# Cross attention on one core: maximum scores in one pair of PSUM banks, read by one VectorE operation of 616 columns, in place of two single banks and operations of 308

## What is computed

```
Q = x @ Wq.T + bq ; K = ctx @ Wk.T + bk ; V = ctx @ Wv.T + bv
scores = Q K^T / sqrt(16) ; attn = softmax(scores) ; context = attn @ V
y = context @ Wo.T + bo + x
out = (y - mean(y)) / sqrt(var(y) + 1e-5) * gamma + beta
```

## Time and profile before

| | us |
|---|---|
| median of three executions | 227.6 |
| profiled execution | 227.75 |
| its span | 225.9 |
| TensorE busy | 203.4 |
| GpSimd busy | 183.9 |
| VectorE busy | 181.3 |
| ScalarE busy | 172.0 |

### The profile page before, as it was taken

How to read it: one execution, slowest core, us unless ns; L and a number is a source line. 1 busy time by engine, 2 the same in 40 slices (tenths; PEclk the granted TensorE clock), 3 DMA queues, 4 the chain that set the end, 5 groups by cost and what they waited for, 6 DMA issues and landing times.

```text
span 225.9 us, 6883 instructions
## 1 busy us (share of the span) xinstructions
PE 203.4 (90%) x2740; PEld 190.3 (84%) x2740; DVE 181.3 (80%) x378; ACT 172.0 (76%) x313; POOL 183.9 (81%) x163
## 2 busy tenths in 40 slices
PE   0999999899999899989999899989998999999830
PEld 0997799799999789988999799969997999998720
DVE  5699977468778978987988888897889788885494
ACT  4589579778879769896889688968896887887530
POOL 9999464786388958997699869985999499999973
PEclk9999999999999999999999999999999999999995
DMA  6947321434721153115321432143124111211022
GB/s 204 328 79 208 63 55 52 149 99 154 201 65 46 49 147 98 51 52 138 94 59 49 128 70 90 52 124 80 50 72 80 46 49 49 78 65 49 0 96 93
DMA packets 24808, 20.96 MB, mean 93 GB/s; under 512 B 10554, under 2 KB 21953, under 8 KB 24776
## 3 DMA queue, kind: packets, MB, share of 16 engines
q1 hardware_dynamic: 23544, 19.26, 30.3%
q10 hardware_dynamic: 1232, 1.26, 1.9%
HBM read 11.32 MB, written 4.19 MB: 69 GB/s over the span
## 4 chain that ended last, share of the span: by engine, by line
POOL 35%; PE 29%; DVE 12%; issue 12%; ACT 8%; DMA 2%; POOLq 0%; DVEq 0%; ACTq 0%
POOL p_l L1046 22%; PE ps_x L348 12%; PE ps_s L348 8%; DVE xT_l L768 6%; PE ps_acc L348 5%; POOL result L1054 5%; POOL x_rows L1063 4%; POOL rs_y L1075 3%; PE ps_d L348 3%; ACT p_h L688 3%; DVE result L909 2%; DMA w_raw<-in_wkT 2%; ACT ctx_h L695 1%; POOL rs_v L1069 1%; DVE vrest L800 1%
## 5 line engine op out<-in xcount | busy, mean ns | idle before, releaser
L1046 POOL TENSOR_TENSOR p_l<-p,p_h 128x512 f16<-128x512 f32 x80 | 100.6, 1264 | 29.0 <-ACT p_h L688 28.1
L854 DVE TENSOR_REDUCE maxima<-ps_d 128x4 f32<-128x308 f32 x128 | 57.2, 465 | 12.0 <-PE ps_d L348 10.8
L687 ACT ACTIVATE p<-ps_s 128x512 f32<-128x512 f32 x80 | 47.5, 594 | 18.0 <-PE ps_s L348 16.9
L348 PE MATMUL ps_s<-q_low,kblk 128*128 128x256 f32 x192 | 47.5, 282 | 1.1 <-issue 1.0
L348 PE MATMUL ps_acc<-vblk,p_h 128*128 128x34 bf16 (+1 forms) x960 | 47.0, 182 | 0.5 <-POOL p_l L1046 0.4
L688 ACT ACTIVATE p_h<-ps_s 128x512 f16<-128x512 f32 x80 | 47.3, 591 | 0.0
L348 PEld LDWEIGHTS ps_acc<-vblk,p_h 128*128 128x128 f16 x960 | 42.6, 96 | 4.8 <-issue 1.9
L348 PE MATMUL ps_acc<-vblk,p_l 128*128 128x34 bf16 (+1 forms) x640 | 45.1, 181 | 0.0
L348 PE MATMUL ps_s<-q_lo,kblk 128*128 128x256 f32 x160 | 45.0, 281 | 0.0
L348 PE MATMUL ps_d<-kblk,q_low 128*128 128x308 f32 x128 | 41.6, 329 | 0.2 <-DVE maxima L854 0.2
L348 PEld LDWEIGHTS ps_acc<-vblk,p_l 128*128 128x128 f16 x640 | 38.7, 96 | 0.0
(11 more groups left out here) (90 smaller groups left out, 458.8 us busy)
## 6 DMA issues: line engine op xcount, KB each, us to landing
xT_raw<-in_xT SPq DMA_DIRECT2D x8, 512.0 KB, 3.9
x_rows<-in_x SPq DMA_DIRECT2D x16, 256.0 KB, 2.9
out_dram<-result SPq DMA_DIRECT2D x15, 256.0 KB, 2.2
kblk<-kT SPq DMA_DIRECT2D x64, 38.5 KB, 2.3
c_raw<-in_cT ACTq DMA_DIRECT2D x4, 308.0 KB, 3.9
vblk<-vparts SPq DMA_DIRECT2D x4, 184.1 KB
rows_sb<-in_bias_rows SPq DMA_DIRECT2D x1, 384.0 KB, 6.4
kblk<-kblk SPq DMA_DIRECT2D x3, 96.0 KB, 2.4
```

What stands on the lines that cost most here:

```text
L348: return nc.tensor.matmul(o, w, m, start=start, stop=stop, skip_group_check=True)
L687: nc.scalar.activation(p32[:, n % P32SLOTS], ps_s[n % 2][:], ACT.Exp, scale=SCALE)
L854: v_.tensor_reduce(maxima[:, t, h0:h0 + DMAX_HEADS], ps_d[((DMAX + 1) * (s + 1) + j) % 2][:, 0:DMAX_HEADS * SKV] .rearrange("p (h k) -> p ...
L1046: g_.tensor_tensor(p_l[:, n % PSLOTS], p32[:, n % P32SLOTS], p_h[:, n % PSLOTS], ALU.subtract).then_inc(rest16, 1)
```

## The change

The two banks become one tile of two banks (ps_d, 128 x 2 x 512). DMAX goes from 8 to 4: for each query tile and half, two matmuls (308 columns each, the same queries) fill both banks back to back, the second one signals, and one VectorE operation reduces the 616 columns to eight maxima. A pair of matmuls waits until the reduction of the pair before is done, since no other bank is left. The table tasks has one entry for all steps: pairs 0, 1, 2 and 3 at (0, 0), (1, 1), (2, 0) and (3, 1). On VectorE reductions 0 and 1 and reductions 2 and 3 of before become one each, ahead of and behind the residual; the third pair comes between the denominators of half 1 and aggregate, the fourth behind the normalization of half 1. In the last output step (s = 16) the second half of the turned context uses the first bank of the pair, and the turned maxima lie there too.

```diff
--- before.py
+++ after.py
@@ -58,7 +58,7 @@
 WIDE = TILES * P
 UNITS = HALVES * TILES // 2
 DMAX_HEADS = HH // 2
-DMAX = QT * HALVES * 2
+DMAX = QT * HALVES
 VW = DK + 1
 VP = 3
 GROUP = 4
@@ -196,7 +196,7 @@
 
         ps_s = [bank(f"ps_s{n}", [P, 2, SQ]) for n in range(2)]
         ps_acc = [bank(f"ps_acc{n}", [P, 512]) for n in range(2)]
-        ps_d = [bank(f"ps_d{n}", [P, 512]) for n in range(2)]
+        ps_d = bank("ps_d", [P, 2, 512])
         ps_x = [bank(f"ps_x{n}", [P, 512]) for n in range(2)]
 
 
@@ -250,7 +250,7 @@
 
         def context_turned(s, f):
 
-            return (ps_d[0], 0) if s == B and f else (ps_x[0], f * SQ)
+            return (ps_d[:, 0], 0) if s == B and f else (ps_x[0][:], f * SQ)
 
 
         low_rows, high_rows = slice(P - MROWS, P), slice(0, MROWS)
@@ -417,31 +417,27 @@
                 s = S.first
                 nb = s + 1
 
-                def max_bank(j):
-                    return ps_d[((DMAX + 1) * nb + j) % 2]
-
                 def max_scores(j):
 
-                    t, f, n = j // 4, j // 2 % 2, j % 2
+                    t, f = divmod(j, HALVES)
                     if j == 0:
                         if nb % 2 == 0:
                             S.wait(pe, ld_k[nb // 2 % 2], 16 * HH, 16 * HH * (5 - nb % 4), by=4)
                             S.wait(pe, q_hi, 1, 3)
-                        S.wait(pe, max_done, DMAX, DMAX)
-                    elif j == 1:
                         S.wait(pe, m_done, 1, 1)
                     else:
-                        S.wait(pe, max_done, DMAX, DMAX + j - 1)
+                        S.wait(pe, max_done, DMAX, DMAX + j)
                     q0 = nb % 2 * SQ + t * P
-                    mm(max_bank(j)[:, 0:DMAX_HEADS * SKV], q_low[nb // 2 % 2][:, f, q0:q0 + P],
-                       kblk[:, nb % KSLOTS, f, 0, n * DMAX_HEADS * SKV:(n + 1) * DMAX_HEADS * SKV],
-                       True, True).then_inc(pe_d, 1)
+                    for n in range(2):
+                        ins = mm(ps_d[:, n, 0:DMAX_HEADS * SKV], q_low[nb // 2 % 2][:, f, q0:q0 + P],
+                                 kblk[:, nb % KSLOTS, f, 0, n * DMAX_HEADS * SKV:(n + 1) * DMAX_HEADS * SKV], True, True)
+                    ins.then_inc(pe_d, 1)
 
                 def turn_maxima():
 
                     S.wait(pe, max_done, DMAX, 2 * DMAX)
                     for t in range(QT):
-                        ins = nc.tensor.transpose(max_bank(DMAX)[0:MROWS, t * P:(t + 1) * P], maxima[:, t, :], ident_sb[:])
+                        ins = nc.tensor.transpose(ps_d[0:MROWS, 0, t * P:(t + 1) * P], maxima[:, t, :], ident_sb[:])
                     ins.then_inc(pe_m, 1)
 
                 def score_tile(u, n):
@@ -541,11 +537,7 @@
 
 
 
-                tasks = {(0, 0): 0, (0, 1): 1, (1, 0): 2, (1, 1): 3, (2, 0): 4, (2, 1): 5, (3, 0): 6, (3, 1): 7,
-                         (4, 1): DMAX}
-                if S.project_q and s > 0:
-                    tasks = {(0, 0): 0, (0, 1): 1, (0, 2): 2, (1, 0): 3, (1, 2): 4, (2, 0): 5, (2, 2): 6, (3, 1): 7,
-                             (4, 1): DMAX}
+                tasks = {(0, 0): 0, (1, 1): 1, (2, 0): 2, (3, 1): 3, (4, 1): DMAX}
                 for u in range(UNITS):
                     for part in range(4):
                         if part < 2 and S.scores:
@@ -702,7 +694,7 @@
                         act.wait_ge(shift_set, 1)
                     nb = s + 1
                     cols = slice(nb % 2 * SQ, (nb % 2 + 1) * SQ)
-                    m = ps_d[((DMAX + 1) * nb + DMAX) % 2][0:MROWS, 0:SQ].unsqueeze(1).broadcast_to([MROWS, HALVES, SQ])
+                    m = ps_d[0:MROWS, 0, 0:SQ].unsqueeze(1).broadcast_to([MROWS, HALVES, SQ])
                     nc.scalar.activation(q_low[nb // 2 % 2][low_rows, :, cols], m, add, bias=shift[low_rows, 0:1])
                     nc.scalar.activation(q_high[nb // 2 % 2][high_rows, :, cols], m, add,
                                          bias=shift[high_rows, 0:1]).then_inc(m_done, 1)
@@ -846,14 +838,13 @@
 
                 def max_of(j):
 
-                    t, f, n = j // 4, j // 2 % 2, j % 2
+                    t, f = divmod(j, HALVES)
                     S.wait(dve, pe_d, DMAX, DMAX + j + 1)
                     if j == 0:
                         S.wait(dve, pe_m, 1, 1)
-                    h0 = f * HH + n * DMAX_HEADS
-                    v_.tensor_reduce(maxima[:, t, h0:h0 + DMAX_HEADS],
-                                     ps_d[((DMAX + 1) * (s + 1) + j) % 2][:, 0:DMAX_HEADS * SKV]
-                                     .rearrange("p (h k) -> p h k", k=SKV), AX.X, ALU.max).then_inc(max_done, 1)
+                    v_.tensor_reduce(maxima[:, t, f * HH:(f + 1) * HH].rearrange("p (n h) -> p n h", n=2),
+                                     ps_d[:, :, 0:DMAX_HEADS * SKV].rearrange("p n (h k) -> p n h k", k=SKV),
+                                     AX.X, ALU.max).then_inc(max_done, 1)
                     if j in between:
                         between[j]()
 
@@ -948,14 +939,12 @@
                 when(S.output, (denominators, 0))
                 when(S.maxima, (max_of, 0))
                 when(S.output, (normalize, 0))
-                when(S.maxima, (max_of, 1))
                 when(s == B, (denominators, 1), (normalize, 1))
                 when(S.norm, (residual,))
                 when(s == B, (context_lo_part, 0))
-                when(S.maxima, (max_of, 2))
+                when(S.maxima, (max_of, 1))
                 if S.norm:
                     S.wait(dve, y_done, 1, -1)
-                when(S.maxima, (max_of, 3))
                 when(S.norm, (statistics, 0))
                 when(S.project_q, (queries, 0))
                 when(s == B, (context_lo_part, 1))
@@ -964,14 +953,11 @@
                 when(s == B - 1, (bias_x,))
                 if S.norm:
                     S.wait(dve, stats_done, QT, -QT)
-                when(S.maxima, (max_of, 4))
+                when(S.maxima, (max_of, 2))
                 when(S.norm, (aggregate,))
-                when(S.project_q, (max_of, 5))
                 when(S.output and s < B, (normalize, 1))
                 when(S.project_q, (queries, 1))
-                when(S.maxima and not S.project_q, (max_of, 5))
-                when(S.maxima, (max_of, 6))
-                when(S.maxima, (max_of, 7))
+                when(S.maxima, (max_of, 3))
                 when(S.output and s < B, (context_lo_part, 0, 1))
                 when(S.norm, (centre, 0), (centre, 1))
                 if S.split_x:
@@ -992,7 +978,7 @@
                 dve.wait_ge(x_hi, 2)
                 split_x()
 
-            step(Step(-1), {1: split_second_x, 3: lambda: (value_rest(3), context_lo(3)), 5: lambda: key_lo(2)})
+            step(Step(-1), {0: split_second_x, 1: lambda: (value_rest(3), context_lo(3)), 2: lambda: key_lo(2)})
             values(2)
             key_lo(3)
             weight_lo(3)
```

## The result

The changed kernel took 231.26 us, the profiled execution included, and the kernel before 227.57 to 227.60 in the runs of the same comparison; the ratio is 1.0161, with a 95% interval from 1.0136 to 1.0185. That is 1.6% slower: less than the 2% that were set as the bound for a change, but well clear of no difference, and 0.7 us over the forecast of 230.6 us. (Both kernels also have executions some 2% longer at a lower granted clock, 0.974 and 0.983 in place of 0.99 for the changed one, and the times and ratios compared from here on leave such executions out.)

What follows compares the result with a forecast made beforehand. TensorE was taken as nearly full and VectorE as having room; -0.2, +0.32 (step 1), +0.37 (step 2), +2.1 (steps 3 to 12) and +0.32 (step 13) make +2.9 us, forecast 230.6 us, 8-in-10 range 227.5 to 233.3.

Steps and rivals of the forecast that it cites:

- up to the start of step 1: Step -1: shorter reductions bring the keys' low part and projection forward, 0.2 us gained; step 0 has no transposes, nothing.
- step 1: Odd step with no later wait as cover: transposes wait for the normalization, 0.32 us paid in full.
- step 2: Even step with no wait ahead to absorb or move: transposes wait for the normalization, +0.37 us.
- steps 3 to 12: Five pairs of an odd and an even step, each +0.42 us from late transposes, together +2.1 us.
- step 13: Odd step with no later wait for xT_l as cover: late transposes cost +0.32 us in full.
- step 14: Its delay falls into TensorE's 0.44 us wait for GpSimd in step 15 and costs nothing.
- The start of the third reduction: On VectorE, a reduction can start some 0.35 us behind the start of its matmul.
- If ctx_l no longer waits for ScalarE in the odd step: Sign of being wrong: VectorE's 0.70 us idle ahead of ctx_l in the odd step would be gone.
- A longer reduction: Longer by x costs 13x at most: x in steps 1, 2, 4, 6, 8, 10, 12, 3x in 13 and 14.
- no change: Rival: waits ahead of the transposes don't arise or the third reduction starts sooner; 227.6 us, chance 0.14.
- faster (VectorE bounds): Rival: VectorE's 3.8 us come off the path, chiefly as less waiting for xT_l; 223.8 us, chance 0.06.
- The slower one: Rival: one operation over two banks takes longer than its columns say; over 2% slower, 233.4 us at 0.90 us, chance 0.20.

Runs made afterwards that it cites:

- experiment 5: Changed kernel with the merging undone, each pair reduced by two operations of 308 columns, all else kept: 232.74, 232.91 and 234.15 us, ratio 1.0227.
- experiment 3: Changed kernel with the normalization of half 1 ahead of the third reduction in odd steps 3 to 11 alone: 231.26 to 231.68 us, ratio 1.0161.
- experiment 2: Changed kernel with the normalization of half 1 ahead of the third reduction in even steps 0 to 12 alone: 227.92 to 230.44 us, ratio 1.0038.
- experiment 1: Changed kernel with the normalization of half 1 ahead of the third reduction and aggregate in every step: 227.03 to 228.20 us, ratio 0.9993.
- experiment 7: Kernel before, unmerged, with the normalization of half 1 moved behind one more reduction on VectorE: 230.47 to 231.15 us, ratio 1.0119.
- Experiment 4: Changed kernel with the normalization of half 1 ahead of the third reduction in step 14 alone: 231.07 to 231.28 us, ratio 1.0148.
- experiment 6: Changed kernel reducing only the first 48 of a head's 77 keys, 384 columns in place of 616: 228.10 to 229.10 us, ratio 1.0023.
- experiment 8: Changed kernel with the normalization ahead of the third reduction in every step and xT_l ahead of centre in odd steps: 230.48 and 231.13 us, ratio 1.0119.

## Why the prediction was right, and where it was off

The mechanism held. TensorE has little room, VectorE has much; the merged operation is priced by its columns (forecast 0.71 us of spacing and 0.79 of duration, measured 0.72 and 0.79) and gives back some 0.06 us a pair, as the gaps of experiment 5 confirm (0.70 against 0.64 us); the transposes wait for a normalization that stands behind it; and the loss of odd steps 3 to 11 is covered by the wait for xT_l (experiment 3) while that of the even ones is paid (experiment 2). Experiments 1 and 7 show the cause from both sides: take the late normalization out of the change and its loss is gone, put it into the kernel before and 2.9 us are lost. Two steps take 23.89 us (138.52 to 162.41), forecast 23.87.

The sum was 2.9 us; the profiled executions differ by 3.5 and their spans by 3.6. Term by term, as forecast and as measured: up to the start of step 1, -0.2 and -0.29; step 1, +0.32 and +0.40; step 2, +0.37 and +0.46; steps 3 to 12, +2.1 and +2.30 (0.57 to 2.87); step 13, +0.32 and +0.39; step 14, nothing and +0.40, of which the last stretch takes back 0.09 to the end of the span. The first term fits by luck: 0.2 us were forecast for step -1 and nothing for step 0, and it was 0.09 ahead of step 0 and 0.20 within it. What gained the 0.20 is open.

- **Step 14** is the term that failed, and the largest part of the difference. I had let its delay fall into TensorE's wait for GpSimd in step 15. That wait is 0.43 us in the trace of the change, as before: what it waits for came later too. Experiment 4 gives some 0.3 us for step 14. The idle time of one engine is cover only if the engine it waits for is not itself delayed.
- **The start of the third reduction and the length of the transposes** are the mis-sized terms in the other steps. I let a reduction start 0.35 us behind its matmul; from step 2 on the third one starts 0.41 us behind it, so the gap ahead of the transposes is 0.51 us longer than normal and not 0.45. And I priced the transposes as before; behind a wait they took 0.41 us in place of 0.36 (143.96 to 144.37). In the even steps that is 0.11 us each: from the start of the query projection to the next odd step it is 12.02 us (150.39 to 162.41), where 11.55 were before, +0.47 and not +0.37. In steps 1 and 13, which are 0.08 and 0.07 off, the transposes start 0.20 us later in the step than before (0.18 forecast) and take 0.05 us longer. In the odd steps 3 to 11 the fault is covered, for xT_l starts 9.50 us after the start of its step, as before (9.51).
- **ctx_l.** "If ctx_l no longer waits for ScalarE in the odd step" stood among the signs that I am wrong, and it came so: the last reduction starts behind transposes that restart late and ends where ctx_l starts. It cost nothing, since ctx_l starts 7.14 us into the step, 7.16 before; but the cover was used up.
- **A longer reduction** costs more than the 13 times of the prediction: 0.055 us a pair cost 1.5 us in experiment 5, because the odd steps are no longer covered and the second pair of matmuls comes late as well. The 0.03 us that the prediction had to spare there were gone in the changed kernel. For a shorter one 13 times 0.245 would be 3.2, and 2.9 was measured, although steps 13 and 14 did not give the three times that this count has.
- **The waits** were forecast at 6.3 us for the transposes and 2.9 for xT_l; the profile shows 4.8 and 2.2. The forecast was a delay from start to start, and the table counts idle time, so the two don't compare: from start to start the gaps are 0.51 us longer a time but for step 1, some 7 us in all, more than forecast.
- The two steps that I read, and called 11 and 12, are 9 and 10; the starts in the table above show it. Nothing in the sum hung on it.

Of the rivals, no change is refuted by the 14 waits and the 4.2 us that experiment 1 gives back; faster (VectorE bounds) is refuted by experiment 6 and by a busy time 6.4 us lower at a longer run. The slower one, an operation dear for crossing two banks, is refuted by its mean of 792 ns. As to the Trainium skill (VectorE: DVE Perf Modes, section on the TRN2 errata): by its cycles 616 columns would take 767 ns, an estimate, and the trace has 792; the spacing gives back 60 ns a pair in place of its 125, so that the measurement decides against the larger saving. The Trainium skill also has the rule to read PSUM in another bank than the one that a running matmul writes (PSUM, Partial Sum Buffer, summary of rules). Having no other bank to write cost at most 0.06 us a time in experiment 1, where the fourth pair of the odd steps starts 0.05 to 0.06 us after the third reduction has ended and up to 0.06 us later than it otherwise would, and 0.82 us a time in experiment 8, where the reductions were late.

## What to carry to other kernels

When operations are merged on an engine with room, look at what stood between the parts: the larger piece pushes back whatever follows it in the same queue, and an operation for which the full engine waits must go ahead of it. Here one line moved made the difference between 231.3 and 227.0 us, and the merging itself gained nothing that could be measured. Measure a wait on TensorE by the start to start of neighbouring matmuls, not by the table of waits alone, and before calling a later wait cover, ask whether what it waits for is delayed too.

## What the runs showed of the hardware

- The idle time in the profile understates what a stop of the matmul stream costs, since a matmul of 256 columns lasts 0.28 us and the next starts 0.12 us after it has begun: 0.35 us idle went with a delay of 0.51 us, and where the table had no wait 0.24 us were lost (experiment 7). Four transposes behind such a stop took 0.41 us in place of 0.36; the extra 0.05 us lies between the first and the second (0.17 in place of 0.11).
- What an operation of VectorE takes depended on what GpSimd ran beside it: centre (128 x 256) took 0.51 to 0.86 us beside the end of result and the start of p_l, the more the longer result ran beside it, 1.38 beside p_l, 1.51 beside x_rows. The GpSimd operation that began while xT_l was under way on VectorE took longer too: p_l 2.15 us in place of 1.16 in experiment 1, x_rows 2.31 in place of 1.47 in experiment 8. Two operations that were moved past each other on VectorE made the centres dearer by 1 us (experiment 8).
- A reduction that waits for its matmul starts 0.34 us after the matmul's start; the third of steps 2 to 14, which waits for a second semaphore too, 0.41 us.
- A reduction over two banks with four levels of addressing took 792 ns for 616 columns, 465 ns for 308 in one bank, and a c_l of 616 columns from SBUF 0.78 us.
